# Wavelet mix on one core: one edge step per synthesis unit, its rows moved by GpSimd transfers, three copies of the projected blocks

## The reference, cut to what matters

```python
B, T, N, D = x.shape                       # 8, 512, 207, 64
sig = x.transpose(0, 2, 3, 1).reshape(-1, T)
a, details = sig, []
for _ in range(3):
    a, d = _dwt(a)                         # 8 taps, stride 2
    details.append(d)
coeffs = [a] + details[::-1]
w = component_weights.reshape(4, D)
enh = [c * w[i][channel] for i, c in enumerate(coeffs)]
rec = enh[0]
for d in enh[1:]:
    rec = _idwt(rec[:, :d.shape[-1]], d)
xr = rec[:, :T].reshape(B, N, D, T).transpose(0, 3, 1, 2)
return x + xr @ proj_w.T + proj_b          # float32
```

## Time and profile before

| | |
|---|---|
| median of 3 runs | 2358.09 us (2357.73 to 2360.01) |
| the profiled execution, its own time | 2359.12 us |
| its span in the profile | 2357.3 us |
| granted TensorE clock, mean | 0.996 |
| PE busy | 99% |
| weight loads (PEld) busy | 93% |
| ACT busy | 78% |
| DVE busy | 74% |
| GpSimd busy | 12% |
| DMA, mean share of 16 engines | about half |

### The profile page before, as it was taken

The page is one execution under the profiler, slowest core; times in us unless marked ns, Lnnn a source line. Parts: engine busy times, 40 slices in busy tenths (PEclk is TensorE's granted clock), DMA queues, the critical chain, the costliest instruction groups (busy, mean ns, idle before and its releaser), DMA issues.

```text
span 2357.3 us, 85222 instructions
## 1 busy us (share of the span) xinstructions
PE 2342.1 (99%) x33980; PEld 2189.6 (93%) x33980; DVE 1750.1 (74%) x2920; ACT 1830.6 (78%) x3938; POOL 284.2 (12%) x1051
## 2 busy tenths in 40 slices
PE   9999999999999999999999999999999999999998
PEld 8999999999999999999999999999999999999987
DVE  5777777777777777777777777777777777777766
ACT  5777777777777777777777777777777777777776
POOL 1111111111111111111111111111111111111110
PEclk9999999999999999999999999999999999999998
DMA  3545454454644645444454644645445454544643
GB/s 127 219 184 191 178 201 173 182 212 162 242 162 162 233 172 199 180 188 186 178 203 170 235 162 162 241 163 210 183 174 198 178 192 182 222 162 167 237 162 122
DMA packets 107209, 439.42 MB, mean 186 GB/s; under 512 B 6801, under 2 KB 8081, under 8 KB 106898
## 3 DMA queue, kind: packets, MB, share of 16 engines
q1 hardware_dynamic: 106144, 434.16, 48.9%
q10 hardware_dynamic: 754, 0.28, 0.0%
HBM read 217.33 MB, written 217.06 MB: 184 GB/s over the span
## 4 chain that ended last, share of the span: by engine, by line
PE 98%; DVE 0%; issue 0%; DMA 0%; ACT 0%; ACTq 0%; DVEq 0%
PE proj_ps L436 31%; PE coefs_ps L382 31%; PE synth_ps L465 12%; PE synth_ps L477 11%; PE synth_ps L488 6%; PE proj_ps L446 2%; PE synth_ps L479 2%; PE synth_ps L467 2%; PE synth_ps L490 2%; DMA edge_sb<-edge_m 0%; DVE x_sb L676 0%; DVE proj_lo L656 0%; DVE coefs_sb L650 0%; ACT stack_sb L602 0%; ACTq L552 0%
## 5 line engine op out<-in xcount | busy, mean ns | idle before, releaser
L382 PEld LDWEIGHTS coefs_ps<-analysis_sb,x_sb 64*128 64x128 f32 x13200 | 945.5, 188 | 102.2 <-DVE coefs_sb L650 53.4
L382 PE MATMUL coefs_ps<-analysis_sb,x_sb 64*128 64x84 f32 x13200 | 1009.9, 270 | 2.7 <-DVE coefs_sb L645 1.5
L436 PE MATMUL proj_ps<-w_sb,coefs_sb 64*128 64x64 f32 x13248 | 871.3, 271 | 1.2 <-issue 1.2
L656 DVE TENSOR_TENSOR proj_lo<-proj_ps,proj_hi 128x512 fp32r<-128x512 f32 x828 | 568.1, 686 | 370.0 <-ACT proj_hi L571 370.0
L436 PEld LDWEIGHTS proj_ps<-w_sb,coefs_sb 64*128 64x128 f32 x13248 | 815.9, 189 | 1.4 <-issue 1.3
L650 DVE TENSOR_TENSOR coefs_sb<-coefs_ps,scale_sb 128x552 f32<-128x552 f32 x825 | 602.4, 730 | 207.6 <-PE coefs_ps L382 206.7
L571 ACT ACTIVATE proj_hi<-proj_ps 128x512 fp32r<-128x512 f32 x828 | 472.1, 596 | 174.6 <-PE proj_ps L446 157.4
L589 ACT ACTIVATE stack_sb<-proj_hi 20x512 fp32r<-20x512 f32 x621 | 390.9, 629 | 209.1 <-DVE proj_lo L656 204.1
L676 DVE TENSOR_TENSOR x_sb<-synth_ps,x_sb 128x512 f32<-128x512 f32 x828 | 531.7, 684 | 16.7 <-PE synth_ps L490 6.9
L341 POOL TENSOR_TENSOR coefs_sb<-coefs_sb 128x20 f32<-128x20 f32 x828 | 187.8, 227 | 1893.4 <-DVE coefs_sb L650 1892.7
L589 ACT ACTIVATE stack_sb<-proj_lo 20x512 fp32r<-20x512 f32 x621 | 390.4, 629 | 15.0
(11 more groups left out here) (58 smaller groups left out, 2849.1 us busy)
## 6 DMA issues: line engine op xcount, KB each, us to landing
x_sb<-x SPq DMA_DIRECT2D x182, 1152.0 KB, 11.7
out<-x_sb SPq DMA_DIRECT2D x182, 1152.0 KB, 6.3
out<-x_sb SPq DMA_DIRECT2D x1, 1280.0 KB, 4.7
x_sb<-x SPq DMA_DIRECT2D x1, 1024.0 KB, 8.5
out<-x_sb SPq DMA_DIRECT2D x2, 512.0 KB, 2.9
x_sb<-x SPq DMA_DIRECT2D x1, 768.0 KB, 5.7
x_sb<-x SPq DMA_DIRECT2D x1, 512.0 KB, 4.0
stack_sb<-bias_parts SPq DMA_DIRECT2D x12, 2.0 KB, 2.7
```

Source lines behind the costliest of these rows:

```text
L382: return lambda cols: nc.tensor.matmul(out[:, at:at + HALF_COLS], x_sb[half_rows[side], w, cols], analysis_sb[half_rows[side], :], start=s ...
L436: mm = nc.tensor.matmul(out_cols[:, :, p, :], coefs_of(g, p)[rows, own_cols(w)], w_sb[rows, rows].rearrange("k (h c) -> k h c", h=2), star ...
L656: nc.vector.tensor_tensor(proj_lo[w][:, :].rearrange(by_node, n=2), proj_of(w)[:, :, 0:NODE_COLS], proj_hi[w][:, :].bitcast(fp32).rearrang ...
```

## The change

- The edge rows, the stack: it now holds, in each half of 64 rows, 20 rows of the high part, the same 20 rows again, 20 rows of the low part and 3 rows of the bias. `edge_all` is one weight with the rounded edge matrix at the first and third block, its rest at the second, and ones at the bias. So one edge step (two matmuls) takes the place of two, in each unit.
- ACT writes only the first of the three blocks (`move_edge`, one instruction for a window, and `copy_tail_high` for the tail). The other two are written by DMAs that GpSimd issues: for each of three windows and the tail one for the high part again and one for the low part, 8 DMAs of 20 rows of 2 KB in a group. Each stack has its own semaphore, and the edge step waits for its four DMAs.
- The tail is turned into one 32-row block: DVE has 4 transposes of 32x128 instead of 2 of 64x128, ACT's copy of it is 20x512 instead of 128x128, GpSimd's split is 20x512 instead of 128x128.
- `proj_hi`, `proj_lo`, `tail_lo` and the stacks exist three times (`SETS`), used in turn by groups.
- Both units of a group are synthesised in the period of the next group: LATE in the first half, EARLY in the second. DVE's additions move along: in a group it adds windows 0 and 1 of the group before the last, and windows 2 and 3 of the last one. The bias goes into the stacks by 6 DMAs instead of 12.
- SP issues a slot's load before it waits for the sums of the slot to be stored, where it was after the store.

The diff, cut to its core:

```diff
-HIGH_AT, LOW_AT = 0, QUAD
-BIAS_AT = HALO_COLS
+HIGH_AT, AGAIN_AT, LOW_AT, BIAS_AT = 0, HALO_COLS, 2 * HALO_COLS, 3 * HALO_COLS
...
+SETS = 3
+TURN_USES = GROUPS // SETS
...
             def split_tail(turn, g):
                 pool.wait_ge(tail_hi_copied, turn * GROUPS + g + 1)
-                nc.gpsimd.tensor_tensor(tail_lo[:, :], tail_sb[:, :], tail_hi[:, :].bitcast(fp32),
+                nc.gpsimd.tensor_tensor(tail_lo[g % SETS][0:HALO_COLS, :], tail_sb[0:HALO_COLS, :],
+                                        stack_of(g, LATE)[0:HALO_COLS, :].bitcast(fp32),
                                         ALU.subtract).then_inc(tail_lo_copied, 1)
...
+            def send_edge(g, u, half, high, low):
+
+                sent = edges_sent[u][g % SETS]
+                for at, source in ((AGAIN_AT, high), (LOW_AT, low)):
+                    rows = slice(half * HALF + at, half * HALF + at + HALO_COLS)
+                    pool.dma_start(stack_of(g, u)[rows, :].bitcast(fp32),
+                                   source[0:HALO_COLS, :].bitcast(fp32)).then_inc(sent, 16)
...
+                    if not (first and g == 0):
+                        await_edge(*behind, 1)
                     seam_ahead(0)
+                    if not (first and g == 0):
+                        send_window(behind[1], 1, EARLY, 1)
+                    await_edge(turn, g, 3)
                     seam_ahead(1)
+                    send_window(g, 2, EARLY, 0)
+                    send_window(g, 3, LATE, 1)
                     split_tail(turn, g)
+                    await_tail(turn, g)
                     seam_ahead(2)
+                    send_tail(g)
                     seam_ahead(3)
...
-                for weight, stop in ((edge_lo[:, :], False), (edge_hi[:, 0, :], True)):
...
+                pe.wait_ge(edges_sent[u][g % SETS], (turn * TURN_USES + (g // SETS + 1)) * EDGE_SENDS)
+                stack = stack_of(g, u)
+                nc.tensor.matmul(synth_ps[1][:, :], edge_all[half_rows[0], :], stack[half_rows[0], :],
+                                 start=False, stop=True, skip_group_check=True)
+                nc.tensor.matmul(synth_ps[0][:, :], edge_all[half_rows[1], :], stack[half_rows[1], :],
+                                 start=False, stop=True, skip_group_check=True).then_inc(synthesised, 1)
...
-                        synthesise_first(*behind, EARLY, [0, 1, 2], False)
+                        synthesise_first(*behind, LATE, [0, 1, 2], opening)
                     second_ahead(1)
...
-                    synthesise_first(turn, g, LATE, [0], first)
+                    if not start:
+                        synthesise_first(*behind, EARLY, [0], False)
                     first_ahead(3)
...
-                for node in range(2):
-                    rows = node_rows[node]
-                    last = nc.vector.transpose(tail_sb[rows, :],
-                                               proj_of(ORDER[1])[rows, node, NODE_COLS:NODE_COLS + PAIRS * QUAD])
+                for q in range(4):
+                    cols = slice(q * PAIRS * QUAD, (q + 1) * PAIRS * QUAD)
+                    last = nc.vector.transpose(tail_sb[:, cols],
+                                               proj_of(ORDER[1])[q * QUAD:(q + 1) * QUAD, q // 2,
+                                                                 NODE_COLS:NODE_COLS + PAIRS * QUAD])
```

188 lines of the change are left out of this document (96 added, 92 removed).

## The result

The changed kernel takes **2467.2 us** (median of four runs, 2459.4 to 2472.2) against 2359.1 us before on the same chip: ratio 1.0456, 95% interval 1.0425 to 1.0487. It is 4.6% slower; I had forecast 2327 us. The profiled execution took 2472.2 us with a span of 2470.4.

The account below looks back on a forecast made before the run. PE was taken as the bound. Per group, -0.45 (edge steps) + 0.34 (pair 3) - 0.05 (pair 0) = -0.16 us, over 206 groups 33 us, +1 at the ends: from 2359.1 to 2327 us, range 2290 to 2660.

Parts of the forecast that it names:

- What bounds the kernel: Whole kernel: PE is the bound, 99% busy and 98% of the chain; DVE's scalings are just in time.
- Edge steps, -0.45 us: PE's synthesis: one edge step fewer in each of two units, 0.23 us each, all on the path; 93 us.
- Transposes, 4 x 0.31 us, +0.34 at pair 3: DVE between scalings of pairs 1 and 2: +0.63 us of transposes, making PE lose 0.34 us at pair 3.
- Pair 0, -0.05: Analysis of the next group's pair 0: half of the 0.11 us lost there goes, -0.05 us a group.
- GpSimd, 6.5 + 6d us with d = 0.59: GpSimd's loop per group, d being one DMA issue: 10.0 us, hidden under PE's period; decides above d = 0.77.
- Rival A: Fourth seam of each group: GpSimd's issues are dear and its loop the bound; +297 us, 2655 us; chance 0.39.
- Landing, "no cost": Edge transfers into the stacks: the tail's, needed last, have 5 us against 4.3 at most; no cost.
- Rival C: Edge step: small transfers queue behind SP's x load and land late; +270 us, 2600 us; chance 0.05.
- The rest. SP's earlier loads cost nothing.: SP's slot loads: issued some 8 groups ahead, landing in 11.7 us, no cost; +1 us at the kernel's ends.
- Both of my signs of being wrong: Profile after: a GpSimd issue over 0.77 us, or transposes not taking what those of twice the height take.

Follow-up runs that it names:

- e22: The changed kernel with loop head at slot 0, window 1's transfers sent earlier, x load one group later and each unit's edge step issued twice: 2483.1 us.
- e13: e9 with two of the four transposes of a group left out after the first group: 2341.0 us.
- e9: The changed kernel with the loop's head at slot 0 and window 1's two transfers issued ahead of GpSimd's addition for pair 0: 2372.1 us.
- e4: The changed kernel without GpSimd's eight transfers in a group and without PE's wait for them: 2458.0 us.
- e1: The changed kernel with SyncE's order as before (store a slot first, then load the slot ahead): 2620.6 us.
- e7: The changed kernel with one more wait on SyncE, so the x load starts a whole group later, loop head unmoved: 2392.8 us.
- e11: The kernel before, with SyncE loading first and one group after the store, so the x load meets PE's back edge: 2458.6 us.
- e8: The kernel before with only SyncE's order of the change (load the slot ahead, then store): 2357.7 us.
- e14: e9 with the edge step of each unit issued twice: 2532.5 us.
- e2: The changed kernel with PE's loop head at instruction slot 0 instead of 144: 2413.3 us.

## Why the prediction was wrong, step by step

*What bounds the kernel.* PE, and just-in-time scalings: right, but not all. I read PE's 99% without asking what brings its instructions. The row was on the page before (q8 is 0.8% of the DMA engines, 297 packets), and the head's slot stood in the code.

*Edge steps, -0.45 us, "all of it is on the path".* This failed inside the group, by less. The matmuls cost 0.23 us a step, but they were also the cover of a scaling. The chain after shows the three analyses of the group that wait, pairs 2, 3 and 0, against 0.41 us for a free one:

```profile
1023.03 0.54 PE coefs_ps L422 x8
...
1026.08 0.64 PE coefs_ps L422 x8
...
1028.59 0.55 PE coefs_ps L422 x8
```

0.13 + 0.23 + 0.14 = 0.50 us lost, against 0.11 before. So the group should gain 0.45 - 0.39 = 0.06 us, and it fell by 0.05. e22 shows the same from the other side: put back, the steps cost 0.10 us.

*Transposes, 4 x 0.31 us, +0.34 at pair 3.* The price was exact (307 ns). The stall is 0.23 instead of 0.34; e13, whose group is 0.23 shorter, confirms that it hangs on this chain.

*Pair 0, -0.05.* Wrong sign: 0.14 instead of 0.11 lost. The cover that went seems to have weighed more than ACT's relief; no run separates the two. *Pair 2* I had not looked at: 0.13 us. My stalls came to 0.40 us where 0.50 were measured, 0.10 x 206 = 21 us of the error.

*GpSimd, 6.5 + 6d us with d = 0.59.* Right, with a cheaper d: an issue takes 0.506 us, the loop 9.5 us by my formula. The split took 1.29 us for my 1.27. Rival A, which had 0.39, is refuted, and the 1 us to the first byte that I had taken from the Trainium skill (page DMA: Bandwidth & Descriptors, latency section) as a possible price is no price of an issue here.

*Landing, "no cost".* Half right. The tail was in time, but I followed only the tail. Window 1's blocks, sent after the next group's first seam, were late in groups in which x or out was in flight: e9 puts their price at 41 us where the head is at slot 0. In the change itself e4 prices all the transfers together at 9 to 12 us. Rival C had the mechanism; its 270 us were far too much. e1, with SyncE's old order, has 87.6 us of direct waits for them.

*"The rest. SP's earlier loads cost nothing."* **This is the step that failed by most.** I asked only whether x would be there in time for PE. The moved load meets the back edge (1072.6 against 1073.1 us), and the first instruction packet behind the branch is taken up 2.9 to 4.6 us after it instead of 0.6 to 1.3. e7 takes the collision away and gains 74 us; e11 gives it to the kernel before and costs 100.

The whole sum closes: nine quiet groups against a turn give 20 x 6.0 = 120 us, and with the 21 us of the stalls 2327 + 21 + 120 = 2468, measured 2467. But 120 us are not all the load's. e7 has 40 of them still: the longer branch, the late transfers of window 1, and a rest. I had priced none of these. So the load alone doesn't carry the sign. Without the collision (e7) the kernel is still 33 us slower than the one before, and with slot 0 and the earlier transfers (e9) 13 us, where I had forecast 32 us less.

The load moved for two reasons that I had both noted and priced at nothing: SyncE's order, and a synthesis half a period later, with which `summed` comes later. e8 has the first alone, in the kernel before: 15 us earlier, and no loss. That the later synthesis then puts it back by the 5.5 us that make it meet the branch is argued, not tested. e1, with the old order in the changed kernel, changed the whole traffic and kept x in flight at the branch.

The range of 2290 to 2660 held the result, but by the width that rival A gave it, not for its reason. Both of my signs of being wrong, an issue over 0.77 us and dearer transposes, stayed away; the sign that came was PE at 88% of the chain where I had asked for 98.

What stays open: why the branch itself takes 3 to 4 us in e1, e14 and e22, and 1 us in the change. The traces show that it is again a packet that is awaited. Wherever a branch took over 0.6 us, it ended 2.3 to 3.0 us after the packet ahead of its end was taken up; e14 and e22 have that packet up to 4.3 us behind the branch's start, the kernel before 2 us ahead of it. Why the packet is that late is not shown. The block that holds the loop's end and the fetch of its head may follow each other too closely there, but no run varied the body's length alone, or the slot with it.

## What to carry to other kernels

When PE is 99% busy, work taken out of it was worth its time here only where it covered nothing: for each engine that is just in time, write down the matmuls between its trigger and its consumer before and after, for all such places and not the tightest alone. The change was worth 0.05 us in a quiet group as it came; with the covers given back (which also wins the 0.11 us that the kernel before lost) the group fell by 0.53 us, 11.18 to 10.65. And when a bulk load moves, compare its time with the loop's back edge: instructions come over the same DMA engines; the cheap tests are to move the load by a group, one wait, or the head to the start of a block, one number.

## What the runs showed of the hardware

- The first instruction packet of 16 KB behind PE's branch was taken up 0.6 to 1.3 us after the branch's end on quiet DMA engines (before), and 2.9 to 4.6 us after it where 1152 KB of x was in flight (after; 3.1 to 4.1 in e11). PE went on 2.3 to 2.7 us after that. It need not stop PE: with the head at slot 0 the packet was as late (e2, 3.7 us in the median), and the kernel took 54 us less.
- An idle of 2.6 us on PE was followed by 4.9 us at half the granted clock, which cost nearly as much again.
- A GpSimd issue of 20 rows of 2 KB took 0.506 us. SyncE's issues took 0.577 at least for the bias rows and 0.466 in the median for its loads of x. The transfer landed in 1.8 us in the median for the tail and 3.7 to 3.9 for windows, up to 8.1.
- A transpose costs the same for 32 partitions (307 ns) as for 64 (0.31).
- Load and store of 1152 KB started together landed in 14.3 and 6.5 us (e1), one after the other in 8.0 and 6.4 (after): the same total, but PE waited 87.6 us for small transfers in the first case and 9.6 in the second.
